# Two feed-forward stages of a one-core kernel: expert and tile numbers are loaded into registers without range checks, and at other places

## The chip, the core and the metric

The kernel runs on one core of a Trainium2 chip. The metric is the device time of one execution in microseconds (us). A core has several engines that run side by side, each with a sequencer that reads its own list of instructions in order: TensorE (PE in the profile; PEld is its loading of weights), VectorE (DVE), ScalarE (ACT), GpSimd (POOL), and SyncE (SP), which only issues transfers. Engines wait for each other by semaphores. A `q` behind an engine's name in the profile (DVEq, PEldq) means its sequencer: what it does by itself, such as arithmetic on registers, and not the engine's data path.

## The reference

Six blocks follow each other on x, an array of 8 x 512 tokens of 128 values: a feed-forward (f), a state-space scan (s), a feed-forward (f), a mixture (m), causal attention (a), and the mixture again (m). The change lies in both feed-forwards, which share weights:

```python
def _L0_ffn_ref(hidden_states, gate_w, w1, b1, w2, b2):
    x = hidden_states.reshape(-1, h)
    gate_probs = jax.nn.softmax(x @ gate_w.T, axis=-1)
    expert_idx = jnp.argmax(gate_probs, axis=-1)
    expert_w = jnp.take_along_axis(gate_probs, expert_idx[:, None], axis=1)[:, 0]
    out = jnp.zeros_like(x)
    for e in range(n_experts):                       # 8
        ye = jax.nn.relu(x @ w1[e] + b1[e]) @ w2[e] + b2[e]
        out = out + jnp.where((expert_idx == e)[:, None], ye * expert_w[:, None], 0.0)
    return out.reshape(b, s, h)
x = x + 0.5 * _L0_ffn_ref(_layernorm(x), ...)
```

Each of the 4096 tokens goes through one of 8 experts, which is known only when the data are there.

## The kernel before

**Sorting.** A feed-forward stage normalises the tokens, writes them to DRAM, computes the gate, and sorts the tokens by expert. The sorted tokens fill 32 tiles of 128. Where a tile holds the tokens of two experts it is worked on twice, so there are 32 + 7 = 39 items, each a pair of an expert and a tile. DVE computes both numbers for all items (`expert_f`, `tile_f`, L646 and L647), writes them as integers to two small rows in SBUF (`expert_of`, `tile_of`) and raises `items_ready` (L649).

**The item loop.** `up(j)` multiplies tile j's tokens by the expert's first weights (four products, L815; each takes two passes, so the profile has eight), `hidden(j)` adds the bias and applies the relu (one quarter on DVE, L671, three on ScalarE, L734), `down(j)` adds the second bias by a product (L823) and multiplies by the second weights (L827), `result(j)` adds the masked product to the sorted results on DVE (L680). DVE also copies each item's first weights to a fixed place, two items ahead (`pick`, L666). `turn_in(t)` transposes a gathered tile (L797), and ScalarE copies it (L724). POOL gathers tiles from DRAM up to eight ahead (`AHEAD`, L853) and scatters finished tiles back by ten items later (L859), one of each in turn, once the loop is under way: gather t waits for the transpose of tile t - 8, and scatter t for the result of item t + 7. When all are scattered, SP reads the rows back and DVE adds them to x (L709).

Each engine has its own order of this, written out by hand: TensorE does `turn_in(j+2)`, `up(j+1)`, `down(j)`; DVE `pick(j+2)`, `hidden(j+1)`, `result(j)`; ScalarE `tokens(j+2)`, `hidden(j+1)`.

**The numbers in registers.** Which weights, bias column and tokens an instruction reads hangs on the item's two numbers, so each engine loads them into registers of its sequencer. `item_values` (L559 to L562) loads four at once, and puts behind the load, for each value, register arithmetic and an assert that it is within 0 and `top`. `choose(j)` calls it when j is a multiple of four, for both numbers on DVE (at the head of `pick`) and on TensorE (at the head of `up`), and for the expert on ScalarE (in `hidden`). With 39 items that is ten times a stage.

The code that the change touches, and what calls it:

Of the kernel before, what the change touches and what calls it, by code (L numbers as in the profile page):

```python
# [17 lines left out]
ALU = mybir.AluOpType  # L18
# [5 lines left out]
T = B * S // P  # L24
# [4 lines left out]
E, F = 8, 512  # L29
FC = F // P  # L30
ITEMS = T + E - 1
# [82 lines left out]
def build(nc, a, consts, rotary, out, xhat_dram, yrow_dram, stages="fsf"):  # L114
    ctx = ExitStack()
    with ctx:
        def sb(name, shape, dt=F32):
            return ctx.enter_context(nc.sbuf_tensor(name, shape, dt))
# [62 lines left out]
        expert_of = sb("expert_of", [1, ITEM_PAD], I32)  # L181
        tile_of = sb("tile_of", [1, ITEM_PAD], I32)
# [232 lines left out]
        def slots_unit_scalar(act):  # L415
            act.wait_ge(mix_set[1], 1)
            nc.scalar.activation(mu_t[:, 1], bank[7][:, 0:SLOTS], ACT.Sqrt).then_inc(mix_set[2], 1)
# [134 lines left out]
        def ffn(n):  # L552

            s, at = ffn_sems, {k: v * stages[:n].count("f") for k, v in FFN_COUNTS.items()}
            stored, gathered, scattered, back = (ffn_rings[k] for k in RING_COUNTS)
            lanes_on_vector = n == 0
            BY_DVE = 1

            def item_values(engine, table, j, top):  # L559

                last = min(j + 4, ITEMS)
                return nc.values_load_multi_w_load_instructions(table[0:1, j:last], engines=[engine.engine], min_val=0, max_val=top)[1]  # L562

            after_finish[n] = lambda dve, g: normalise_vector(dve, n, s, at, g, stored, at["stored"])
            for k, counts in RING_COUNTS.items():
# [16 lines left out]
            def vector(dve):  # L582
                chain = Chain(dve, s["v"], chains["f"])
# [8 lines left out]
                top, esum, prob, first, dest, lane, row, at_token = (r_t[:, k, :] for k in range(8))  # L592
# [42 lines left out]
                expert_f, tile_f, at_row, expert_at = (item_f[:, k, :] for k in range(4))  # L635
# [9 lines left out]
                nc.vector.tensor_scalar(token_of[:], at_token, -1.0, None, ALU.add).then_inc(s["gather_ready"], 1)  # L645
                chain(nc.vector.tensor_reduce(expert_f, item_cmp[:], AX.X, ALU.add))  # L646
                chain(nc.vector.tensor_tensor(tile_f, number, expert_f, ALU.subtract))  # L647
                nc.vector.tensor_copy(expert_of[:, 0:ITEMS], expert_f[0:1, :])
                nc.vector.tensor_copy(tile_of[:, 0:ITEMS], tile_f[0:1, :]).then_inc(s["items_ready"], 1)  # L649

                dve.wait_ge(s["items_ready"], at["items_ready"] + 1)
                picked = {}
                placed = {}

                def choose(j):
                    if j % 4 == 0:
                        for k, e in enumerate(item_values(dve, expert_of, j, E - 1)):
                            picked[j + k] = e
                        for k, t in enumerate(item_values(dve, tile_of, j, T - 1)):
                            placed[j + k] = t  # L660

                def pick(j):
                    choose(j)
                    if j >= 2:
                        dve.wait_ge(s["h_mm"], at["h_mm"] + j - 1)
                    nc.vector.tensor_copy(w1_tile[:, j % 2, :], w1[:, bass.ds(picked[j], 1), :]).then_inc(s["w1_ready"], 1)  # L666
# [6 lines left out]
                    last.then_inc(s["hT_ready"], 1)  # L673

                def result(j):
                    dve.wait_ge(s["y_mm"], at["y_mm"] + j + 1)
                    if j:
                        dve.wait_ge(s["y_ready"], at["y_ready"] + j)
                    rows = y_sorted[:, bass.ds(placed[j] * D, D)]
                    nc.vector.scalar_tensor_tensor(rows, bank[6 + j % 2][:, 0:D], item_mask[:, j:j + 1], rows,  # L680
                                                   ALU.mult, ALU.add).then_inc(s["y_ready"], 1)

                dve.wait_ge(w1_in, 16)
                pick(0)
                pick(1)
                chain(nc.vector.tensor_scalar(at_row, tile_f, float(P), cst[:, C_P1:C_P1 + 1], ALU.mult, ALU.add))
                chain(nc.vector.tensor_tensor(item_cmp[:], over_items(starts), over_breaks(at_row), ALU.is_lt))
# [25 lines left out]
            def scalar(act):  # L713
                normalise_scalar(act, n, s, at, stored, at["stored"])
                act.wait_ge(s["one_ready"], at["one_ready"] + 1)
                nc.scalar.activation(r_log[:], r_exp[:], ACT.Exp).then_inc(s["exp_ready"], 1)
                if n == 0 and "s" in stages:
                    scan_setup_scalar(act)
                if n == early:
                    slots_unit_scalar(act)  # L720

                def tokens(t):
                    act.wait_ge(s["g_turned"], at["g_turned"] + t + 1)
                    nc.scalar.copy(xgT[:, t * P:t * P + P], bank[t % 2][:, 0:P]).then_inc(s["xgT"], 1)  # L724

                picked = {}

                def hidden(j):
                    if j % 4 == 0:
                        for k, e in enumerate(item_values(act, expert_of, j, E - 1)):  # L730
                            picked[j + k] = e
                    act.wait_ge(s["h_mm"], at["h_mm"] + j + 1)
                    for c in range(BY_DVE, FC):
                        last = nc.scalar.activation(hidT[:, j % 2, c, :], bank[4 + j % 2][:, c * P:c * P + P], ACT.Relu,  # L734
                                                    bias=b1T[:, bass.ds(picked[j] * FC + c, 1)])
                    last.then_inc(s["hT_ready_a"], 1)

                if not lanes_on_vector:
                    act.wait_ge(s["row_hot"], at["row_hot"] + 1)
                    nc.scalar.activation(tile_hot[:, 1], tile_hot[:, 2], ACT.Copy, scale=cst[:, C_P1:C_P1 + 1]).then_inc(s["lanes_ready"], 1)  # L740
                act.wait_ge(s["items_ready"], at["items_ready"] + 1)
                tokens(0)
                tokens(1)
                hidden(0)
                for j in range(ITEMS):
                    if j + 2 < T:
                        tokens(j + 2)
                    if j + 1 < ITEMS:
                        hidden(j + 1)

            def tensor(pe):
                if n == stages.index("f"):
                    pe.wait_ge(placed_w, 1)
                for i in range(GROUPS):
# [4 lines left out]
                    for h in range(2):  # L759
                        pe.wait_ge(s["xT_ready"], at["xT_ready"] + 2 * i + h + 1)  # L760
                        for k in range(TB):
                            last = pe.matmul(bank[2][:, (8 * i + 4 * h + k) * E:(8 * i + 4 * h + k + 1) * E], xT[:, h, k * P:k * P + P],  # L762
                                             gateT[:], start=True, stop=True)
# [14 lines left out]
                for t in range(T):  # L778
                    pe.wait_ge(s["hot_ready"], at["hot_ready"] + t + 1)
                    last = pe.matmul(bank[2][:, 0:2 * T], lane_hot[:, t, :], tile_hot[:, 0:2, t, :], start=(t == 0), stop=(t == T - 1))  # L780
# [9 lines left out]
                picked = {}  # L790
                placed = {}
# [4 lines left out]
                        pe.wait_ge(s["xgT"], at["xgT"] + t - 1)  # L796
                    pe.transpose(bank[t % 2][:, 0:P], xg[:, t % AHEAD, :], ident).then_inc(s["g_turned"], 1)  # L797

                def choose(j):
                    if j % 4 == 0:  # L800
                        for k, e in enumerate(item_values(pe, expert_of, j, E - 1)):
                            picked[j + k] = e
                        for k, t in enumerate(item_values(pe, tile_of, j, T - 1)):
                            placed[j + k] = t

                def up(j):
                    choose(j)
                    pe.wait_ge(s["w1_ready"], at["w1_ready"] + j + 1)
                    pe.wait_ge(s["xgT"], at["xgT"] + min(j + 1, T))
                    if j >= 2:  # L810
                        pe.wait_ge(s["hT_ready"], at["hT_ready"] + j - 1)
                        pe.wait_ge(s["hT_ready_a"], at["hT_ready_a"] + j - 1)
                    tokens = xgT[:, bass.ds(placed[j] * P, P)]
                    for c in range(FC):
                        last = pe.matmul(bank[(2 if c < BY_DVE else 4) + j % 2][:, c * P:c * P + P], w1_tile[:, j % 2, c * P:c * P + P], tokens,  # L815
                                         start=True, stop=True)
                    last.then_inc(s["h_mm"], 1)

                def down(j):
                    e = picked[j]  # L820
                    if j >= 2:
                        pe.wait_ge(s["y_ready"], at["y_ready"] + j - 1)
                    pe.matmul(bank[6 + j % 2][:, 0:D], ones3[:], b2rows[:, bass.ds(e * D, D)], start=True, stop=False)  # L823
                    pe.wait_ge(s["hT_ready"], at["hT_ready"] + j + 1)
                    pe.wait_ge(s["hT_ready_a"], at["hT_ready_a"] + j + 1)
                    for c in range(FC):
                        last = pe.matmul(bank[6 + j % 2][:, 0:D], hidT[:, j % 2, c, :], w2[:, bass.ds(e, 1), c, :],  # L827
                                         start=False, stop=(c == FC - 1))
                    last.then_inc(s["y_mm"], 1)
# [11 lines left out]
            def gpsimd(pool):  # L841
# [23 lines left out]
                for j in range(T + LATER):  # L865
                    if j + AHEAD < T:
                        gather(j + AHEAD)
                    if j >= LATER:
                        scatter(j - LATER)

            return dict(sync=sync, vector=vector, scalar=scalar, tensor=tensor, gpsimd=gpsimd)


# [1055 lines left out]
```

## Time and profile before

| | us |
|---|---|
| median of 3 runs | 1026.81 (1023.82 to 1027.28) |
| the profiled execution | 1027.21 |
| its span, of which all shares are | 1025.5 |
| TensorE products busy | 770.5 (75%) |
| DVE busy | 631.1 (62%) |
| ScalarE busy | 523.9 (51%) |
| POOL busy | 419.4 (41%) |
| item loop of the first stage, first up product to last scatter's start | 65.79 to 170.38 |
| item loop of the second stage | 282.93 to 389.32 |

The busy time of an engine counts operations on data only. What a sequencer does by itself shows as idle time of its engine, with "issue" as what ended it where the engine waited for no other, and has rows of its own when one asks for the source line. In brackets behind a row of the timeline stands how long the engine had been idle before it and who ended that. A number such as x8 is how many instructions the row merges.

### The profile page before, as it was taken

How to read it: one execution, taken by the hardware profiler on the slowest of the kernel's cores; microseconds unless marked ns; L12 is line 12 of the kernel's file. 1: busy time of each engine (PE TensorE's matmuls, PEld its weight loads, DVE VectorE, ACT ScalarE, POOL GpSimd, SP SyncE). 2: the span in 40 equal slices, each digit the busy share in tenths (PEclk: the TensorE clock that was granted, in tenths of full speed). 3: DMA queues.
4: the chain of work that ended last, by engine and by line, in shares of the span. 5: the costliest groups of instructions: out<-in, count | busy, mean ns of one | idle time of the engine just before them, and what ended most of it. 6: DMA issues, size and time to landing. Idle time of an engine off the chain costs nothing.

```text
span 1025.5 us, 18801 instructions
## 1 busy us (share of the span) xinstructions
PE 770.5 (75%) x5550; PEld 513.1 (50%) x5550; DVE 631.1 (62%) x2289; ACT 523.9 (51%) x1435; POOL 419.4 (41%) x537
## 2 busy tenths in 40 slices
PE   4768775698378871299784788899899899829977
PEld 3658774457278771177571223333333333317757
DVE  4544333866743346955378677777768787466634
ACT  5324432505134431766611267667667677677660
POOL 2055733301146532411136575675674834251100
PEclk9999998696589996599895579899889999959998
DMA  5731103002011103000003532321422400000002
GB/s 150 233 87 35 53 24 83 21 1 83 10 38 44 41 27 93 1 1 1 2 20 43 63 48 33 48 44 33 54 37 31 64 4 2 3 1 1 1 1 82
DMA packets 52530, 42.03 MB, mean 41 GB/s; under 512 B 9224, under 2 KB 48080, under 8 KB 52432
## 3 DMA queue, kind: packets, MB, share of 16 engines
q1 hardware_dynamic: 46784, 31.74, 15.7%
q0 software_dynamic: 4096, 8.40, 2.8%
q8 instruction: 48, 0.79, 0.3%
q10 hardware_dynamic: 1552, 0.70, 0.3%
q14 instruction: 50, 0.41, 0.1%
HBM read 17.35 MB, written 10.49 MB: 27 GB/s over the span
## 4 chain that ended last, share of the span: by engine, by line
PE 49%; DVE 19%; issue 9%; ACT 8%; POOL 7%; DVEq 4%; DMA 2%; ACTq 1%; SPq 0%; POOLq 0%
PE psum L815 6%; PE psum L827 6%; PE psum L1525 5%; DVEq L562 4%; PE psum L1296 3%; PE psum L1259 3%; PE psum L762 3%; PE psum L1268 3%; DVE half_stats L447 3%; DVE cst L1592 2%; PE psum L1510 2%; DVE x L709 2%; PE psum L1465 2%; PE psum L1359 2%; PE psum L758 2%
## 5 line engine op out<-in xcount | busy, mean ns | idle before, releaser
L1592 DVE CUSTOM_DVE_ANT_0 cst<-psum,rot 128x512 bf16<-128x512 f32 (+3 forms) x512 | 219.0, 487 | 70.5 <-PE psum L1497 61.4
L1654 ACT ACTIVATE arena<-psum 128x512 f32<-128x512 f32 (+1 forms) x384 | 178.3, 530 | 56.2 <-PE psum L1510 50.4
L1497 PE MATMUL psum<-arena 48*128 48x512 bf16 (+3 forms) x512 | 122.2, 330 | 17.0 <-DVE row_max L1592 11.3
L734 ACT ACTIVATE arena<-psum,gate_b1T 128x128 f32<-128x128 f32 x234 | 69.0, 365 | 118.2 <-PE psum L815 118.2
L1510 PE MATMUL psum<-arena 51*128 51x512 bf16 (+3 forms) x512 | 114.8, 315 | 13.7 <-ACT arena L1654 7.1
L815 PE MATMUL psum<-arena 128*128 x624 | 90.2, 291 | 46.4 <-DVE arena L671 33.0
L853 POOL DMA_INDIRECT arena<-xhat_rows,token_of x64 | 62.3, 974 | 121.3 <-DVE token_of L645 81.0
L815 PEld LDWEIGHTS psum<-arena 128*128 128x128 f32 x624 | 81.5, 204 | 51.0 <-issue 51.0
L1525 PE MATMUL psum<-arena 128*32 128x512 f32 (+3 forms) x1024 | 98.7, 484 | 7.6 <-POOL arena L1752 7.6
L1749 POOL TENSOR_SCALAR_AFFINE_SELECT arena<-arena 128x384 f32<-128x384 f32 x128 | 63.6, 521 | 97.5 <-ACT arena L1654 97.5
L827 PE MATMUL psum<-arena 128*128 x624 | 89.0, 287 | 0.5 <-ACT arena L734 0.5
L859 POOL DMA_INDIRECT result_rows<-arena,token_of x64 | 62.9, 983 | 62.6 <-DVE arena L680 50.8
L827 PEld LDWEIGHTS psum<-arena 128*128 128x128 f32 x624 | 78.1, 197 | 2.0 <-issue 0.9
L1510 PEld LDWEIGHTS psum<-arena 51*128 51x128 bf16 x512 | 38.5, 96 | 80.0 <-ACT arena L1654 45.7
L1497 PEld LDWEIGHTS psum<-arena 48*128 48x128 bf16 x512 | 38.9, 98 | 63.1 <-DVE row_max L1592 50.5
L666 DVE COPY arena<-arena 128x512 f32 x78 | 33.1, 426 | 59.1 <-issue 59.1
L469 ACT ACTIVATE st<-st 128x8 f32<-128x8 f32 x24 | 4.9, 208 | 113.2 <-DVE st L461 113.1
L680 DVE SCALAR_TENSOR_TENSOR arena<-psum,item_mask,arena 128x128 f32 x78 | 27.2, 349 | 41.2 <-PE psum L827 41.1
L1252 PE MATMUL psum<-cst,xh 128*128 128x128 f32 x64 | 10.6, 292 | 53.0 <-POOL xh L1136 53.0
L671 DVE TENSOR_SCALAR arena<-psum,gate_b1T 128x128 f32<-128x128 f32 x78 | 27.3, 350 | 36.1 <-PE psum L815 36.0
L1136 POOL TENSOR_TENSOR xh<-arena,st 128x512 f32<-128x512 f32 x16 | 18.9, 1184 | 69.3 <-PE psum L1252 67.5
L447 DVE BATCH_NORM_STATS2 half_stats<-x 128x6 f32<-128x128 f32 x192 | 39.4, 278 | 7.2 <-DMA x<-in_L_attn_x 6.4
(248 smaller groups left out, 1648.3 us busy)
## 6 DMA issues: line engine op xcount, KB each, us to landing
arena<-cut SPq DMA_DIRECT2D x192, 64.0 KB
xhat_rows<-xh SPq DMA_DIRECT2D x16, 256.0 KB, 2.3
arena<-result_rows SPq DMA_DIRECT2D x8, 512.0 KB, 6.0
x<-in_L_attn_x SPq DMA_DIRECT2D x4, 512.0 KB, 7.7
arena<-in_L_ffn_w SPq DMA_DIRECT2D x1, 2048.0 KB, 10.1
out<-x SPq DMA_DIRECT2D x4, 512.0 KB, 3.2
arena<-xhat_rows,token_of POOLq DMA_INDIRECT x64, 2.5
result_rows<-arena,token_of POOLq DMA_INDIRECT x64, 2.3
```

Source lines behind the costliest of these rows:

```text
L447: nc.vector.bn_stats(half_stats[:, t, :], x[:, t, :]).then_inc(stat_sem, 1)
L734: last = nc.scalar.activation(hidT[:, j % 2, c, :], bank[4 + j % 2][:, c * P:c * P + P], ACT.Relu, bias=b1T[:, bass.ds(picked[j] * FC + c, ...
L815: last = pe.matmul(bank[(2 if c < BY_DVE else 4) + j % 2][:, c * P:c * P + P], w1_tile[:, j % 2, c * P:c * P + P], tokens, start=True, sto ...
L827: last = pe.matmul(bank[6 + j % 2][:, 0:D], hidT[:, j % 2, c, :], w2[:, bass.ds(e, 1), c, :], start=False, stop=(c == FC - 1))
L853: pool.indirect_dma_start(xg[:, t % AHEAD, :], None, xhat_dram, bass.IndirectOffsetOnAxis(token_of[:, t:t + 1], 0)).then_inc(gathered[t % ...
L859: pool.indirect_dma_start(yrow_dram, bass.IndirectOffsetOnAxis(token_of[:, t:t + 1], 0), y_sorted[:, t * D:t * D + D], None).then_inc(scat ...
L1497: mm = pe.matmul(to[:, col:col + (k + 1) * P], q_stack[b % STACKS][rows, h, k * P:k * P + P], k_stack[b % STACKS][rows, h, 0:(k + 1) * P], ...
L1510: mm = pe.matmul(bank[MAX_BANKS + number % EXP_BANKS][:, col:col + S - k * P], k_stack[b % STACKS][rows, h, k * P:k * P + P], q_stack[b % ...
L1525: last = pe.matmul(bank[6][32 * j:32 * j + 32, k * P:], v_aug[b % 2][:, k, HALF * a + h, :], prob_e[g % 2][:, j, E_AT[k]:E_AT[k] + S - k * ...
L1592: last = nc.vector.tensor_tensor_reduce(masked_scores[:, number % 2, col:col + n_keys], frm[:, col:col + n_keys], mask[:, S - n_keys:], 1. ...
L1654: nc.scalar.activation(prob_e[g % 2][:, j, first:last], bank[MAX_BANKS + number % EXP_BANKS][:, 0:last - first], ACT.Exp, scale=DH ** -0.5 ...
L1749: pool.affine_select(blocks, blocks, pattern=[[0, 3], [1, P]], compare_op=ALU.is_ge, fill=0.0, base=0, channel_multiplier=-1)
```

## The change

The loads are made with the option that leaves the checks out. For that, tile numbers are clamped to 0 to 31 by one more operation on DVE before they are stored. And the two numbers are loaded at different places: `choose_expert` where j is a multiple of four, `choose_tile` at j = 0 (two values) and then where j mod 4 is 2 (four). On DVE experts are loaded in `pick` as before and tiles in `result`; on TensorE tiles in `up` and experts in `down`; on ScalarE experts in `hidden` as before.

```diff
-            def item_values(engine, table, j, top):
-                last = min(j + 4, ITEMS)
-                return nc.values_load_multi_w_load_instructions(table[0:1, j:last], engines=[engine.engine], min_val=0, max_val=top)[1]
+            def item_values(engine, table, j, last, top):
+                return nc.values_load_multi_w_load_instructions(
+                    table[0:1, j:min(last, ITEMS)], engines=[engine.engine], min_val=0, max_val=top,
+                    skip_runtime_bounds_check_because="an expert is a count of 7 comparisons and a tile is clamped to 0..31 before it is stored")[1]
+            def choose_expert(engine, picked, j):
+                if j % 4 == 0:
+                    for k, e in enumerate(item_values(engine, expert_of, j, j + 4, E - 1)):
+                        picked[j + k] = e
+            def choose_tile(engine, placed, j):
+                if j == 0 or j % 4 == 2:
+                    for k, t in enumerate(item_values(engine, tile_of, j, j + 4 if j else 2, T - 1)):
+                        placed[j + k] = t
...
                 chain(nc.vector.tensor_tensor(tile_f, number, expert_f, ALU.subtract))
+                chain(nc.vector.tensor_scalar(tile_f, tile_f, 0.0, float(T - 1), ALU.max, ALU.min))
...
                 def pick(j):
-                    choose(j)
+                    choose_expert(dve, picked, j)
...
                 def result(j):
+                    choose_tile(dve, placed, j)
                     dve.wait_ge(s["y_mm"], at["y_mm"] + j + 1)
...
                 def up(j):
-                    choose(j)
+                    choose_tile(pe, placed, j)
                     pe.wait_ge(s["w1_ready"], at["w1_ready"] + j + 1)
...
                 def down(j):
+                    choose_expert(pe, picked, j)
                     e = picked[j]
```

The order of instructions shows what stands on the engines. A TENSOR_LOAD is a load of registers, an ISA row register arithmetic or an assert. TensorE before, around up(4): the transpose, both loads with their checks, the up products, the bias product of the item before.

```order
L797 MATMUL psum<-cst,arena 128x128
L562 TENSOR_LOAD expert_of
L562 ISA x8
L562 TENSOR_LOAD tile_of
L562 ISA x8
L815 ISA
L815 MATMUL psum<-arena 128x128 x4
L823 ISA
L823 MATMUL psum<-arena,ones 128x128
```

TensorE in the changed kernel, from up(5) to up(6): experts ahead of the bias product of down(4), tiles ahead of the up products of item 6. Lines of the code are one less for L815 and six more for L797.

```order
L814 ISA
L814 MATMUL psum<-arena 128x128 x4
L561 TENSOR_LOAD expert_of
L823 ISA
L823 MATMUL psum<-arena,ones 128x128
...
L803 MATMUL psum<-cst,arena 128x128
L561 TENSOR_LOAD tile_of
L814 ISA
L814 MATMUL psum<-arena 128x128 x4
```

The 16 ISA rows are gone, and the two loads stand at two places of the loop, two items apart in what they are for. DVE before, around pick(8): both loads, then copy, relu and result.

```order
L562 TENSOR_LOAD expert_of
L562 ISA x8
L562 TENSOR_LOAD tile_of
L562 ISA x8
L666 ISA
L666 COPY arena<-arena 128x512
L671 ISA
L671 TENSOR_SCALAR arena<-psum,gate_b1T 128x128
L680 ISA
L680 SCALAR_TENSOR_TENSOR arena<-psum,item_mask,arena 128x128
```

DVE in the changed kernel at the same place: the copy is L673 here, the relu L678, the result L688.

```order
L561 TENSOR_LOAD expert_of
L673 ISA
L673 COPY arena<-arena 128x512
L678 ISA
L678 TENSOR_SCALAR arena<-psum,gate_b1T 128x128
L561 TENSOR_LOAD tile_of
L688 ISA
L688 SCALAR_TENSOR_TENSOR arena<-psum,item_mask,arena 128x128
```

The experts are still loaded ahead of the copy, and the tiles have moved behind the relu, ahead of the result's wait for the down products.

## Rows read from the trace of the kernel before

**Rows 1.** chain of waits, 44 to 420 us, shares by line

```profile
by line: PE psum L815 17.1%; PE psum L827 15.9%; DVEq L562 10.0%; issue 8.7%; DVE x L709 5.1%; DVE half_stats L447 4.0%; PE psum L762 3.7%; PE psum L939 3.1%; PE psum L758 2.3%; DMA arena<-result_rows 2.2%; DVE arena L680 1.9%; DMA arena<-x
```

**Rows 2.** source line L562: ns min/median/max, first and last start

```profile
L562 DVEq FUSED_REGOPS  x156: 183/183/216, 58.9 to 380.2; - x156
...
L562 DVEq TENSOR_LOAD <-expert_of x20: 339/343/805, 58.3 to 376.8; - x20
```

**Rows 3.** timeline: start us, us, what, [idle before <-releaser]

```profile
93.65 0.35 DVE L680 SCALAR_TENSOR_TENSOR arena<-psum,item_mask,arena 128x128 f32 x1 [0.63 <-PE psum L827]
...
96.79 0.43 DVE L666 COPY arena<-arena 128x512 f32 x1 [2.79 <-issue]
...
97.72 1.15 PE L815 MATMUL psum<-arena 128*128 x8 [2.10 <-DVE arena L671]
...
99.82 1.06 PE L815 MATMUL psum<-arena 128*128 x8
...
100.02 0.35 DVE L680 SCALAR_TENSOR_TENSOR arena<-psum,item_mask,arena 128x128 f32 x1 [0.63 <-PE psum L827]
...
101.83 1.06 PE L815 MATMUL psum<-arena 128*128 x8
```

**Rows 4.** sequencers on L562, L823 and L827, 92.65 to 94.6 us

```profile
L562 DVEq TENSOR_LOAD <-expert_of x1: 343/343/343, 93.7 to 93.7; - x1
...
L562 PEldq TENSOR_LOAD <-expert_of x1: 329/329/329, 94.3 to 94.3; - x1
...
L823 PEldq FUSED_REGOPS  x1: 60/60/60, 92.7 to 92.7; - x1
...
L827 PEldq FUSED_REGOPS  x4: 46/51/60, 93.7 to 94.1; - x4
```

**Rows 5.** first loop's start: timeline, and TensorE's sequencer on L562

```profile
62.31 0.27 ACT L724 COPY arena<-psum 128x128 f32<-128x128 f32 x1 [2.39 <-PE psum L797]
...
L562 PEldq TENSOR_LOAD <-expert_of x1: 529/529/529, 62.3 to 62.3; - x1
...
65.79 2.07 PE L815 MATMUL psum<-arena 128*128 x8 [3.05 <-issue]
...
70.41 1.06 PE L815 MATMUL psum<-arena 128*128 x8
```

**Rows 6.** timeline, end of the first stage's item loop

```profile
162.22 1.15 PE L815 MATMUL psum<-arena 128*128 x8 [2.65 <-DVE arena L666]
...
164.21 1.06 PE L815 MATMUL psum<-arena 128*128 x8
...
166.10 1.06 PE L815 MATMUL psum<-arena 128*128 x8
...
170.38 0.97 POOL L859 DMA_INDIRECT result_rows<-arena,token_of  x1 [0.47 <-DVE arena L680]
```

**Rows 7.** POOL's timeline (gathers 18, 31, scatter 14), and the page's issues

```profile
89.88 0.94 POOL L853 DMA_INDIRECT arena<-xhat_rows,token_of  x1 [3.58 <-PE psum L797]
...
123.67 0.97 POOL L853 DMA_INDIRECT arena<-xhat_rows,token_of  x1 [0.30 <-issue]
...
126.23 0.98 POOL L859 DMA_INDIRECT result_rows<-arena,token_of  x1 [0.30 <-issue]
...
arena<-xhat_rows,token_of POOLq DMA_INDIRECT x64, 2.5
```

**Rows 8.** timeline of TensorE, second stage

```profile
282.93 2.07 PE L815 MATMUL psum<-arena 128*128 x8 [2.83 <-issue]
...
288.18 1.06 PE L815 MATMUL psum<-arena 128*128 x8
...
381.15 1.15 PE L815 MATMUL psum<-arena 128*128 x8 [2.64 <-DVE arena L666]
```

**Rows 9.** busy time by stretch (PE, PEld, DVE, ACT, POOL), granted clock, DMA share

```profile
283.00:300.00 17.00, 14.80 (x98) 14.41 (x99) 7.62 (x18) 6.28 (x23) 9.14 (x10) 0.77 0.14 37
...
320.00:345.00 25.00, 20.75 (x184) 20.17 (x183) 10.53 (x31) 11.66 (x42) 18.45 (x20) 1.00 0.17 51
```

More of the change, by code:

```diff
@@ L653, in vector @@
                 placed = {}
[L655 to L660, printed above, removed]
                 def pick(j):
-                    choose(j)
+                    choose_expert(dve, picked, j)
                     if j >= 2:
@@ L728, in hidden @@
                 def hidden(j):
-                    if j % 4 == 0:
-                        for k, e in enumerate(item_values(act, expert_of, j, E - 1)):
-                            picked[j + k] = e
+                    choose_expert(act, picked, j)
                     act.wait_ge(s["h_mm"], at["h_mm"] + j + 1)
@@ L797, in turn_in @@
                     pe.transpose(bank[t % 2][:, 0:P], xg[:, t % AHEAD, :], ident).then_inc(s["g_turned"], 1)
[L799 to L804, printed above, removed]
                 def up(j):
-                    choose(j)
+                    choose_tile(pe, placed, j)
                     pe.wait_ge(s["w1_ready"], at["w1_ready"] + j + 1)
```

## The prediction, made before the changed kernel ran

> **What bounds the kernel now.** I read the page's chain first, then the chain of waits of the first part of the span (44 to 420 us), which holds both feed-forward stages, then the timeline inside one stage, then the sequencer's rows of the load's line. The chain [rows 1] gives 17.1% to the up products (L815), 15.9% to the down products (L827) and 10.0% to DVE's sequencer on L562, the register load. So TensorE sets the pace, and is stopped by something that is no computation. The timeline [rows 3] shows it: the up products of items start 2.01 us apart (99.82, 101.83), and once in four items there is a hole: DVE idles 2.79 us "issue" before its weight copy at 96.79, TensorE 2.10 us before 97.72.
>
> The load's line says what fills the hole [rows 2]. On DVE one value costs 183 ns of FUSED_REGOPS (plus an assert), and the load itself, of up to four values, costs 343 ns in the median, 805 at most. Eight values and two loads make 8 x 0.18 + 2 x 0.34 = 2.2 us, and small gaps between ten-odd sequencer instructions the rest of the 2.79. TensorE's sequencer goes through the same list at the same time (its load starts at 94.3, one of DVE's at 93.7 [rows 4]), so its 2.10 us of idleness has two causes side by side, and both must go. ScalarE has half of the list (experts alone) and waits for the same up products as DVE; it can only come nearer to being early.
>
> **What the change removes.** Behind the load nothing is left but the load: 8 x 2 instructions less per four items on DVE and TensorE, 8 on ScalarE. DVE loads its experts before the weight copy and its tiles before a result two items later; TensorE its tiles before up(4m+2) and its experts before down(4m). What is left over is one load of some 0.34 us at each of four places, and each needs a cover.
>
> - TensorE, tiles before up(4m+2). The place in the queue is the old one, behind the down products and a transpose; there the sequencer arrived at 94.3 [rows 4], and while the array ran out of work only at 97.72 - 2.10 = 95.6 [rows 3]. The queue is 1.3 us ahead there; I set aside 0.5 for the address and the dispatch, 0.8 are left, and a load of 0.33 fits.
> - TensorE, experts before down(4m). The sequencer had the address of the bias product ready at 92.7 and then stood until 93.7, when the relu values came and L827's addresses follow [rows 4]. One load fits into that 1.0 us.
> - DVE, tiles before result(4m+2). DVE waits 0.63 us for the down products before L680 (at 100.02 [rows 3]), and its sequencer starts a load some 0.05 us after the operation ahead of it has started (93.65 and 93.7 [rows 3, 4]). Covered.
> - DVE, experts before the weight copy. Not covered on DVE itself: the copy starts one load later than in an item without one. From the result's start at 93.65 it would be 0.05 + 0.34 for the load, some 0.15 for the address, and 0.43 for the copy: it ends at 94.6, and TensorE wants it at 95.6. So it costs nothing; the bounds are 0 and 0.34 x 18 = 6 us, and I take 0.
> - The clamp on DVE is one operation of the size of its neighbours, with its chain wait some 0.2 us, ahead of the event that lets the engines load. TensorE has to wait for gather 0 at that time, until its transposes can run, and the first token copy stands at 62.31 [rows 5]. Cost 0, of at most 0.2 in each stage.
>
> The Trainium skill, DMA: Bandwidth & Descriptors, section "Latency and other measured facts", gives a tensor_load a floor of about 600 ns. The trace disagrees here: 343 ns median, though single loads took 805 ns [rows 2]. With 600 ns at each place the covers on TensorE (0.8 and 1.0 us) would still hold and the sum stay, only with less to spare.
>
> **The sum.** Stage 1. At the start TensorE's first load begins at 62.3 and takes 0.53 us [rows 5]; with no checks and one load up(0) starts at about 62.3 + 0.53 + 0.3 = 63.1 instead of 65.79 (0.3 for address and dispatch is an estimate): 2.7 us. Then from up(0) to up(36). Now: 162.22 - 65.79 = 96.4 us [rows 5, 6]. After: up(0) to up(2) as now, 70.41 - 65.79 = 4.6 (the first products run at half speed, 2.07 us for eight against 1.06); 28 items of 2.005 us = 56.1; six without a transpose at 166.10 - 164.21 = 1.89, 11.3. Together 72.0, which is 24.4 less. What follows up(36) stays as it is. 27.1 us for the stage.
>
> Stage 2. 381.15 - 282.93 = 98.2 us [rows 8]; after: 288.18 - 282.93 = 5.25, and the same 56.1 + 11.3: 72.7, 25.5 less. At the start TensorE idled 2.83 us "issue" before up(0), all but 0.1 to 0.2 of it goes: 2.7. 28.2 us.
>
> In these 55 us lie 2 x 9 holes of some 2.4 us (43), the two starts (5.4), and 6.9 from products that run at 1.2 instead of 2.4 GHz after a hole, from the few loads that took 0.8 us, and from longer first products behind a hole (1.15 against 1.06 us [rows 3]): the granted clock is 0.77 in 283:300, where the loop starts and has its first hole [rows 9]. Nothing in the loop lets TensorE idle afterwards, so I count these as gone.
>
> Is something else late next? POOL. It issues one gather and one scatter per item at 2.6 us ((123.67 - 89.88) / 13) [rows 7], slower than TensorE's 2.005, and only the surplus of gathers made before keeps it from being the bound. After the change up(2) is at 67.7 and up(9) at 81.7. Gather 18 waits for the transpose of tile 10, just before up(9), and starts 0.55 us after it: 82.2. Gather 31 starts 13 x 2.6 later, at 116.0, and has landed by about 119.5 (0.97 to issue and 2.5 to land [rows 7]); its transpose stands before up(30), at 67.7 + 56.1 = 123.8. TensorE never waits for it, with 4.3 us to spare. The scatters: number 14 starts 2.56 us after gather 31 (123.67 and 126.23 [rows 7]), 118.6, and 17 more at 1.28 put the last at 140.4 at the earliest. TensorE ends the last up at 67.7 + 56.1 + 8 x 1.89 = 138.9, and the last scatter follows 170.38 - 166.10 = 4.3 later [rows 6], at 143.2. So the results decide, not POOL, by 2.8 us. In stage 2 the distances are alike. Without this bound the gain is complete; with it at its worst it would lose little.
>
> Sum: 27.1 + 28.2 = 55.3 us. The profiled execution took 1027.2 (span 1025.5), 0.4 above the median of 1026.8. 1027 - 55 = **972 us**. Everything behind the stages (reads of the rows, the scan, the mixing, attention) waits for the stage's end and shifts.
>
> **The rivals.**
> - A load is not covered. Then TensorE stands at each: 38 loads inside the loops at 0.4 us give 15 back, 987. For it: single loads take 0.8 us [rows 2]. Against it: sequencer and array run 1 us apart [rows 4]. The skill's floor of 600 ns would bring this case nearer.
> - POOL becomes the bound. If pairs took 2.9 instead of 2.6 us and scatters 1.5, the last scatter would be 3.9 + 3.6 later, less the 2.8 to spare: about 5 us a stage, 982. For it: 2.6 us a pair is little more than the operations themselves, POOL hardly rests between gathers 18 and 31 [rows 7]; against it: the two margins.
> - The slow stretches stay, because the clock falls at other times as well: of the 6.9 us in the sum that are neither holes nor starts, 5 would stay, 977.
> - Slower than before: TensorE runs at half clock for long. An item at 1.2 GHz costs 1.7 us more (eight products 2.07 against 1.06 less overlap, twice an item). Where more than 55 / 1.7 = 32 of the 78 items did so, the gain would be used up; with all of them it is 1027 - 55 + 78 x 1.7 = 1104. For it: the granted clock of 0.77 in one stretch. Against it: in 320:345, with only 2 us holes, it is 1.00 [rows 9]. The Trainium skill, TensorE: Matmul & The Clock Gate, Part 1, says that throttled is the default and that activity releases it; by that a loop without holes is the safer one.
> - The change does not do what it says: the sequencer spends its time on the load although the checks are gone. The order shows the rows gone, and the load has its own row, so this is small: 1025.
>
> **How the numbers follow.** Forecast 0.78 (its own range 968 to 978), an uncovered load 0.07, POOL 0.07, slow stretches 0.05, half clock 0.02, no effect 0.01. The range of 966 to 984 takes in the first, the slow stretches, POOL, and loads of which most are covered; what is left out is about 1 in 10. About 0.3% is what a measurement of this kernel can tell from no change, so faster has 0.97, same 0.01, slower 0.02.
>
> **What would show it.** In the profile after: no FUSED_REGOPS and no assert on the load's line, about 20 fewer microseconds "issue" before the weight copy per stage; up products 2.0 us apart throughout; up(0) at about 63.1; the last scatter of stage 1 at about 143 instead of 170.38, that of stage 2 about 55 us earlier than now; DVE's sequencer gone from the chain; POOL with only its waits for results at the tail. I am wrong if up products wait for gathers, if the granted clock falls in the loop, or if four-item periods stand well above 8.0 us.

## The result, and the profile after

| | before | changed |
|---|---|---|
| median, us | 1027.05 (4 runs) | 977.23 (975.62 to 979.56, 4 runs) |
| ratio | | 0.9514, 95% interval 0.9473 to 0.9555 |
| profiled execution, span | 1025.5 | 975.4 |
| last scatter of stage 1 starts | 170.38 | 147.71 |
| last scatter of stage 2 starts | 389.32 | 342.75 |

The kernel became 50 us faster; forecast were 55, to 972. In the chain that ended last, on the page of the changed kernel, DVE's sequencer has 0%, against 4% before:

```profile
PE 54%; DVE 15%; ACT 9%; POOL 7%; issue 7%; DMA 3%; SPq 2%; ACTq 1%; DVEq 0%; POOLq 0%
```

The timeline of TensorE in the changed kernel, in the middle of the first stage (start, duration, what, idle time before), is to be read against [rows 3]:

```profile
84.89 1.15 PE L814 MATMUL psum<-arena 128*128 x8 [0.15 <-issue]
...
86.99 1.06 PE L814 MATMUL psum<-arena 128*128 x8
...
89.00 1.06 PE L814 MATMUL psum<-arena 128*128 x8
...
91.00 1.06 PE L814 MATMUL psum<-arena 128*128 x8
...
93.41 1.15 PE L814 MATMUL psum<-arena 128*128 x8 [0.24 <-issue]
```

The hole of 2.10 us is gone, but four items take 93.41 - 84.89 = 8.52 us and not the forecast 4 x 2.005 = 8.02. A hole of 0.24 us has stayed, "issue", and the first products behind it take 1.15 us, not 1.06. It stands ahead of the up products of items 4m+2, where the tiles are now loaded. The rows of the load's line say why (duration min/median/max in ns, the first and last start):

```profile
L561 PEldq TENSOR_LOAD <-tile_of x22: 308/1007/1137, 61.8 to 337.7; - x22
...
L561 DVEq TENSOR_LOAD <-tile_of x22: 317/968/1077, 66.9 to 340.7; - x22
...
L561 DVEq TENSOR_LOAD <-expert_of x20: 340/342/754, 58.5 to 332.9; - x20
...
L561 PEldq TENSOR_LOAD <-expert_of x20: 329/332/774, 63.6 to 336.1; - x20
```

Against [rows 2, 4] the loads of experts are what they were. Those of tiles take three times as long, on both engines; before they were as short as those of experts:

```profile
L562 PEldq TENSOR_LOAD <-tile_of x20: 327/333/772, 64.0 to 379.0; - x20
...
L562 DVEq TENSOR_LOAD <-tile_of x20: 340/352/797, 60.1 to 378.8; - x20
```

The load in front of the hole at 93.41 has this row on TensorE's sequencer in the changed kernel:

```profile
L561 PEldq TENSOR_LOAD <-tile_of x1: 1011/1011/1011, 91.9 to 91.9; - x1
```

It began 1.3 us before the array ran out of work, at 93.41 - 0.24 = 93.17, as in [rows 3, 4], and took 1.01 us; the rest is the way from the load's end to the first product, some 0.5 us. The landmarks of the stage, POOL's included:

```profile
62.76 2.07 PE L814 MATMUL psum<-arena 128*128 x8 [0.51 <-ACT arena L732]
...
68.06 1.15 PE L814 MATMUL psum<-arena 128*128 x8 [0.22 <-issue]
...
83.01 0.94 POOL L853 DMA_INDIRECT arena<-xhat_rows,token_of  x1 [1.06 <-PE psum L803]
...
116.62 1.00 POOL L853 DMA_INDIRECT arena<-xhat_rows,token_of  x1 [0.30 <-issue]
...
119.22 1.15 POOL L859 DMA_INDIRECT result_rows<-arena,token_of  x1 [0.30 <-DVE arena L688]
...
147.71 0.97 POOL L859 DMA_INDIRECT result_rows<-arena,token_of  x1 [0.47 <-DVE arena L688]
...
342.75 0.97 POOL L859 DMA_INDIRECT result_rows<-arena,token_of  x1 [0.47 <-DVE arena L688]
```

up(0) started at 62.76 (forecast 63.1). POOL ran as forecast: gather 18 at 83.01 (82.2), gather 31 at 116.62 (116.0), scatter 14 at 119.22 (118.6), and the last scatter waits for DVE's result, not for POOL. The granted clock was 1.00 over the item loop of stage 1, from the first up products on (busy time of PE, PEld, DVE, ACT and POOL, then the clock, as in [rows 9]):

```profile
63.00:148.00 85.00, 81.80 (x693) 78.72 (x693) 40.61 (x115) 43.43 (x148) 58.18 (x60) 1.00 0.17 50
```

### The profile page after: what moved, and what is told of

It reads as the page before. It is cut to its first block, busy times and chain, and to the rows that moved or that the text cites. A ratio compares the mean times of both kernels' runs of the same rounds, so it can differ in the third digit from the quotient of the medians.

```text
span 975.4 us, 18027 instructions
## 1 busy us (share of the span) xinstructions
PE 764.3 (78%) x5550; PEld 507.5 (52%) x5550; DVE 633.9 (65%) x2291; ACT 523.8 (54%) x1435; POOL 419.5 (43%) x537
## 4 chain that ended last, share of the span: by engine, by line
PE 54%; DVE 15%; ACT 9%; POOL 7%; issue 7%; DMA 3%; SPq 2%; ACTq 1%; DVEq 0%; POOLq 0%
PE psum L814 8%; PE psum L827 7%; PE psum L1525 5%; PE psum L1296 3%; PE psum L1259 3%; PE psum L768 3%; PE psum L1268 3%; DVE cst L1592 3%; PE psum L1510 2%; DVE half_stats L447 2%; DVE x L717 2%; PE psum L1359 2%; PE psum L1465 2%; PE psum L1497 2%; ACT arena L1654 2%
## 5 line engine op out<-in xcount | busy, mean ns | idle before, releaser
L1525 PE MATMUL psum<-arena 128*32 128x512 f32 (+3 forms) x1024 | 98.3, 482 | 6.7 <-POOL arena L1752 6.7
L814 PE MATMUL psum<-arena 128*128 x624 | 87.8, 286 | 4.9 <-issue 2.8
L827 PE MATMUL psum<-arena 128*128 x624 | 86.7, 282 | 0.5 <-ACT arena L740 0.5
L814 PEld LDWEIGHTS psum<-arena 128*128 128x128 f32 x624 | 78.9, 199 | 9.8 <-issue 9.6
L827 PEld LDWEIGHTS psum<-arena 128*128 128x128 f32 x624 | 75.8, 192 | 1.8 <-issue 0.9
L688 DVE SCALAR_TENSOR_TENSOR arena<-psum,item_mask,arena 128x128 f32 x78 | 27.3, 351 | 52.8 <-PE psum L827 52.8
L678 DVE TENSOR_SCALAR arena<-psum,gate_b1T 128x128 f32<-128x128 f32 x78 | 27.2, 349 | 28.2 <-PE psum L814 25.9
L1592 DVE DVE_READ_ACCUMULATOR2_ANT row_max<- 128x1 f32 x512 | 42.5, 83 | 0.0
```

The costliest lines, as they stand in the source:

```text
L1525: last = pe.matmul(bank[6][32 * j:32 * j + 32, k * P:], v_aug[b % 2][:, k, HALF * a + h, :], prob_e[g % 2][:, j, E_AT[k]:E_AT[k] + S - k * ...
L1592: last = nc.vector.tensor_tensor_reduce(masked_scores[:, number % 2, col:col + n_keys], frm[:, col:col + n_keys], mask[:, S - n_keys:], 1. ...
```

## The experiments

Four questions: why the tile loads became slow, what each half of the change is worth, whether two engines' checks really hide behind each other, and what a load costs. Medians are of 4 runs each (10 for e7, one run for e8), and the median of before on the same chips was 1026.5 to 1026.6. The up products are L813, L814 or L815, by the kernel. The diffs show the lines that matter, with "..." where others are left out.

**e1: the row of tiles two words later.** Nothing moves in any order; both rows are made four words longer.

```diff
-        expert_of = sb("expert_of", [1, ITEM_PAD], I32)
-        tile_of = sb("tile_of", [1, ITEM_PAD], I32)
+        expert_of = sb("expert_of", [1, ITEM_PAD + 4], I32)
+        tile_of = sb("tile_of", [1, ITEM_PAD + 4], I32)
...
-                nc.vector.tensor_copy(tile_of[:, 0:ITEMS], tile_f[0:1, :]).then_inc(s["items_ready"], 1)
+                nc.vector.tensor_copy(tile_of[:, 2:2 + ITEMS], tile_f[0:1, :]).then_inc(s["items_ready"], 1)
...
-                    table[0:1, j:min(last, ITEMS)], engines=[engine.engine], min_val=0, max_val=top,
+                    table[0:1, j + at_word:min(last, ITEMS) + at_word], engines=[engine.engine], min_val=0, max_val=top,
```

The added argument `at_word` is 2 for tiles and 0 for experts.

> The changed kernel, but the row of tile numbers is stored two words later, so that the loads of four tiles begin at a multiple of four words instead of two words past one. Nothing is moved in any engine's order. Theory (where a load begins): the loads of four tiles cost 0.33 to 0.35 us on TensorE and DVE instead of 1.0, the up products of four items stand 8.0 us apart instead of 8.4 to 8.55, and the time is about 8 us less than the changed kernel's 977, near 969. Rival (the place of the load, beside a busy array and a busy DVE, makes it slow): the loads stay at 1.0 us and the time at 977. A second rival (POOL takes over as soon as the holes go): loads of 0.34, but up products or the last scatter wait for POOL, 972 to 975.

Measured: 967.9 (967.1 to 969.0), ratio to before 0.9428 (0.9386 to 0.9469). The load's line of e1:

```profile
L561 PEldq TENSOR_LOAD <-tile_of x22: 312/330/728, 62.0 to 329.3; - x22
...
L561 DVEq TENSOR_LOAD <-tile_of x22: 337/342/536, 67.2 to 332.6; - x22
```

And its timeline:

```profile
92.01 1.06 PE L814 MATMUL psum<-arena 128*128 x8
...
100.03 1.06 PE L814 MATMUL psum<-arena 128*128 x8
...
143.55 0.97 POOL L859 DMA_INDIRECT result_rows<-arena,token_of  x1 [0.48 <-DVE arena L688]
...
334.61 0.96 POOL L859 DMA_INDIRECT result_rows<-arena,token_of  x1 [0.48 <-DVE arena L688]
```

Loads of 0.33 and 0.34 us, four items in 8.02 us, no hole. So it was not the place of the load in the order that made it slow, but its first word; e2 leaves the rows where e1 has them and moves the experts' first word alone. e1 is the fastest kernel of this study, 9.3 us ahead of the changed one, whose four runs all lie above its four. POOL as the next bound did not appear: the last scatter follows the last result, at 143.55, where the prediction had it (143.2).

**e2: both rows two words later,** so that tiles are loaded from multiples of four and experts are not.

```diff
-                nc.vector.tensor_copy(expert_of[:, 0:ITEMS], expert_f[0:1, :])
+                nc.vector.tensor_copy(expert_of[:, 2:2 + ITEMS], expert_f[0:1, :])
```

> As the one before, but the row of expert numbers is stored two words later as well, so that now its loads of four begin two words past a multiple of four words, and the tiles' do not. Theory (where a load begins): tile loads 0.34 us, expert loads 1.0 us on TensorE, DVE and ScalarE; TensorE's has about 1.0 us of cover and DVE's about 1.0, so the time is 969 to 975. Rival (the place): expert loads stay at 0.33, tile loads at 1.0, 977. If the slow thing is the row of tiles itself, its loads are at 1.0 too.

Measured: 970.9 (970.5 to 971.8). The slowness changed sides with the offset:

```profile
L561 PEldq TENSOR_LOAD <-tile_of x22: 312/336/720, 61.7 to 332.6; - x22
...
L561 DVEq TENSOR_LOAD <-expert_of x20: 794/966/1212, 58.4 to 328.1; - x20
...
L561 PEldq TENSOR_LOAD <-expert_of x20: 765/1003/1131, 63.5 to 330.9; - x20
```

ScalarE's loads of experts went from 0.31 to 0.91 us as well. Nine loads of four became slow in each stage on each of three engines (the tenth is of three values). They cost 3 us here, over e1, and nine slow tile loads on two engines cost 9 us in the changed kernel: at the experts' places there is more cover.

**e3: no checks, both loads together where they stood before.**

```diff
-                if j == 0 or j % 4 == 2:
+                if j % 4 == 0:
...
                 def pick(j):
                     choose_expert(dve, picked, j)
+                    choose_tile(dve, placed, j)
...
                 def up(j):
+                    choose_expert(pe, picked, j)
                     choose_tile(pe, placed, j)
...
```

> No checks and the clamp as in the changed kernel, but both loads stand together where they stood before the change, ahead of the weight copy on DVE and of the up products on TensorE, every fourth item, and begin at multiples of four words. Theory (where a load begins): loads of 0.34 us; two of them are 0.7 us against about 0.8 us of cover on TensorE, so holes of 0 to 0.2 us per four items, 969 to 973: taking the loads apart is worth nothing and costs by its offset. Rival (taking apart is what covers them): holes of 0.4 us or more, 977 or above.

Measured: 974.8 (974.7 to 975.9), ratio 0.9491 (0.9449 to 0.9532). That is between the two expectations (969 to 973, and 977 or above).

```profile
89.13 1.14 PE L815 MATMUL psum<-arena 128*128 x8
...
97.28 1.15 PE L815 MATMUL psum<-arena 128*128 x8
```

Four items take 8.15 us, 0.13 more than in e1, by a start that comes a little late and longer first products; no idle time shows before them. e3 is no slower than the changed kernel: its median is 2.4 us lower, but the runs of the two overlap. Leaving out the checks alone, with the clamp in their place, brings 51.7 us. Taking the loads apart brought nothing as it was done, and 7 us once the tiles begin at a multiple of four (e1).

**e4: checks on, loads taken apart** as in the changed kernel (the option that leaves them out is dropped from the load).

> The changed kernel with the checks behind the loads again; the loads stay taken apart. On TensorE a tile load is then 1.0 + 8 instructions of register work and asserts, about 1.75 us against about 0.8 of cover, an expert load 0.33 + 0.75 against 1.0. Theory (checks and loads cost what their rows show): a hole of 0.9 to 1.3 us per four items, 985 to 995, so of the 50 us gained the move alone would have brought some 35 and the checks the rest. Rival (the checks are all that matters): 1020 or more.

Measured: 1072.9 (1072.0 to 1075.4), ratio 1.0454 (1.0406 to 1.0501): 46 us slower than before. The theory (985 to 995) missed by far. The rival's number, 1020 or more, held, but not its reason: had the checks been all that matters, the time would have come back to that of before, not 46 us over it. The half of the change that brings nothing without checks does harm with them. **e5** is e4 with the offset of e1, to see how much of it is slow loads.

> The kernel of e4 (checks on, loads taken apart) with the row of tiles stored two words later, so that all loads of four cost 0.34 us. e4 took 1072.9, against an expectation of 985 to 995. Theory one (short pieces fit, and only the 1.0 us loads made e4 slow): each piece is 0.34 + 0.75 us on TensorE against 0.8 to 1.0 of cover and 0.34 + 0.85 on DVE, holes of 0.1 to 0.6 us at places, 975 to 1000. Theory two (taken apart, the checks stop DVE, then TensorE, one after the other instead of side by side, and the array falls to its slow clock more often): 1030 to 1060 even with short loads.

Measured: 1040.5 (1038.9 to 1042.9), ratio 1.0146 (1.0119 to 1.0172). Short loads take away 32 of the 46 us, and with them it is still slower than before, within theory two's range. Not all of the 32 is waiting for loads. TensorE's granted clock, which was 1.00 in the changed kernel's loop, fell in both, more in e4. The loop of stage 1 behind its first products, in e5 and then in e4:

```profile
68.00:176.00 108.00, 87.98 (x670) 78.75 (x668) 38.69 (x112) 41.98 (x143) 53.72 (x55) 0.97 0.12 36
...
68.00:193.00 125.00, 96.47 (x675) 86.95 (x673) 37.50 (x113) 42.12 (x144) 54.09 (x55) 0.90 0.11 31
```

Stage 2's loop has the same clock in each: 0.90 in e4 (250 us in both loops together) and 0.97 in e5 (217 us). As an estimate from these, 25 us of full-speed time are missing in e4 and 7 in e5, so up to 18 of the 32 us came by way of the clock. The timeline of DVE and TensorE in e5 around one item 4m+1:

```profile
98.48 0.35 DVE L687 SCALAR_TENSOR_TENSOR arena<-psum,item_mask,arena 128x128 f32 x1 [1.19 <-issue]
...
98.98 0.43 DVE L672 COPY arena<-arena 128x512 f32 x1
...
99.55 1.15 PE L813 MATMUL psum<-arena 128*128 x8
...
101.35 0.23 PE L822 MATMUL psum<-arena,ones 128*128 x1 [0.65 <-issue]
...
104.13 1.15 PE L813 MATMUL psum<-arena 128*128 x8 [1.27 <-DVE arena L672]
```

And two rows of its sequencer on the load's line at that place (count, ns, first and last start):

```profile
L561 PEldq TENSOR_LOAD <-expert_of x1: 329/329/329, 99.7 to 99.7; - x1
...
L561 PEldq TENSOR_LOAD <-tile_of x1: 331/331/331, 102.2 to 102.2; - x1
```

DVE's checks of tiles hold its result back (98.48, 1.19 us "issue") and with it the weight copy at 98.98. It ends at 99.41, and the up products start at 99.55, as soon as it is there: the sequencer has no lead. It then begins the expert load at 99.7 and is through with its checks at 101.2; the array idles 0.65 us before L822. The products of down(4m) follow, and at 102.2 comes the tile load with its checks, 1.5 us more: a hole of 1.27 us. The row names the weight copy, but that had ended at 103.60, 0.53 us before, and the last check only at about 103.65. Before the change both lists ran at one time on both engines, and made one hole of 2.1 us; in this stretch DVE's and TensorE's stand behind each other. How much of the time that is, e9 and e10 are to tell.

**e6 and e7: checks on one engine alone, loads together** (e3 with the option dropped for DVE, or for TensorE).

> Both loads together at the old place, checks off on TensorE and ScalarE, on on DVE alone (e3 with DVE's checks back). Theory (side by side: DVE's 2.8 us and TensorE's list run at the same time, the longer one sets the hole): DVE's list still delays the weight copy and the relu, so a hole of 1.9 to 2.1 us per four items stays, 1012 to 1026. Rival (the two lists add up): about half of e3's gain of 52 us, 1000.

> The mirror of the one before: checks on TensorE alone, off on DVE and ScalarE. Theory (side by side): TensorE's sequencer arrives 1.3 us ahead of the array and needs 2.7 + 0.4 us for its list, so the hole is 1.8 to 2.0 us, 1008 to 1024. Rival (adds up): 1000.

Measured: e6 1018.4 (1017.7 to 1018.8), ratio 0.9924 (0.9900 to 0.9948); e7 1025.2 (1022.9 to 1028.4), 0.9990 (0.9972 to 1.0008). Taking the checks from TensorE is worth 8 us, taking them from DVE nothing that can be told, and both together 52. Side by side is right, though e7 lies 1 us above the theory's 1008 to 1024. Two reservations. ScalarE's checks are off in e6, e7 and e3 alike, and no run has them off alone; in the kernel before, all 118.2 us that ScalarE idled ahead of its relus ended on TensorE's up products, so they were not what it waited for. And the clock takes part: it is 0.97 to 0.98 over the loops behind the first products before, in e6 and in e7, and 1.00 in e3, which by the estimate above is some 5 of the 52 us. In e6 DVE holds the copy back and TensorE waits for it:

```profile
103.06 0.43 DVE L674 COPY arena<-arena 128x512 f32 x1 [2.77 <-issue]
...
103.63 1.15 PE L815 MATMUL psum<-arena 128*128 x8 [1.72 <-DVE arena L674]
```

In e7 the copy is early, and TensorE's own sequencer makes the same hole:

```profile
104.89 0.43 DVE L674 COPY arena<-arena 128x512 f32 x1 [0.54 <-PE psum L815]
...
108.08 1.15 PE L815 MATMUL psum<-arena 128*128 x8 [2.12 <-issue]
```

**e9 and e10: checks on one engine alone, loads apart and at multiples of four** (e1 with the option dropped for one engine).

> The kernel of e1 (unchecked, apart, all loads of four at a multiple of four words, 967.9) with the checks back on DVE alone. e5, with them on all three engines, took 1040.5, 72.6 more. Theory (shared cover: the array lives on the lead of TensorE's sequencer, DVE's pieces of 1.3 us eat some of it, TensorE's pieces the rest, and only both together break it): 970 to 985, and this and the next kernel together have far less than 72 us of excess. Rival (each engine's pieces cost by themselves): about 36 of excess here, 1004.

> The mirror of the one before: checks back on TensorE alone, at its two places, 1.1 us each against covers of 0.8 and 1.0 us. Theory (shared cover): holes of 0.1 to 0.5 us, 970 to 985. Rival (each by itself): 1004.

Measured: e9 990.6 (990.4 to 991.2), ratio 0.9650 (0.9625 to 0.9676), 22.7 over e1; e10 1000.9 (1000.1 to 1002.8), ratio 0.9755 (0.9728 to 0.9783), 33.0 over it. Together 55.7 of the 72.6 of e5. So most of it is each engine by itself: e10 is near the rival's 1004, e9 between the theory and the rival, and my shared cover as the main cause fell. Some 17 us are left for what the lists do together. They have no run of their own, and two more things lie in them: ScalarE's checks, on in e5 alone (3.1 us of ScalarE's idle time there ended on its own sequencer), and the clock, which over the loops is 1.00 in e9 and e10 against 0.97 in e5, about 7 us by the estimate above.

What I had missed is that on TensorE the two places are neighbours: experts ahead of down(4m), then its products, then tiles ahead of up(4m+2). Rows of e10, TensorE and its sequencer:

```profile
L561 PEldq TENSOR_LOAD <-expert_of x1: 330/330/330, 94.4 to 94.4; - x1
...
96.00 0.23 PE L823 MATMUL psum<-arena,ones 128*128 x1 [0.20 <-issue]
...
L561 PEldq TENSOR_LOAD <-tile_of x1: 330/330/330, 96.8 to 96.8; - x1
...
98.78 1.15 PE L814 MATMUL psum<-arena 128*128 x8 [1.26 <-DVE arena L673]
```

The expert list is through at 95.8 and costs a hole of 0.20 us itself. The tile list begins at 96.8, and the array runs out of work at 98.78 - 1.26 = 97.52: a lead of 0.7 us, where it was 1.3 in the changed kernel at the same place. The tile list then takes 1.5 us with its gaps, where I had reckoned 1.1. So part of the second hole, about 0.5 of the 1.26 us, is lead that the first list had used. No run has the checks at one of TensorE's two places alone.

**e8: single loads measured.** 45 loads more on ScalarE behind the first stage's item loop, from the row of experts, with a copy that uses one value of each.

```diff
+                for v in [nc.values_load_multi_w_load_instructions(expert_of[0:1, 8:12], engines=[act.engine], min_val=0, max_val=E - 1, skip_runtime_bounds_check_because='an expert')[1][-1] for _ in range(3 if n == 0 else 0)]:
+                    nc.scalar.copy(probed[:, bass.ds(next(probe_at), 1)], cst[0:1, bass.ds(v, 1)])
...
```

> The kernel of e1 with 45 more register loads on ScalarE after the first stage's item loop, three each of: four values from word 0, 1, 2, 3 and 6 past a multiple of four, one value from word 0 and 1, two from 0, 1, 2 and 3, three from 0, 1, 2 and 3, each followed by a copy of one value, which leaves the kernel's results as they are. Theory (a load that lies within one piece of four words is fast, one that goes over its end is slow): fast (0.3 us) for four from 0, one from 0 or 1, two from 0, 1 or 2, three from 0 or 1; slow (0.9 to 1.0) for four from 1, 2, 3 and 6, two from 3, three from 2 and 3. Rival (any load that doesn't begin at a multiple of four words is slow): also slow one from 1, two from 1 and 2, three from 1. Second rival (a slow load costs by its values: one access of some 0.25 for each): three from 2 costs 0.25 less than four from 2.

Measured: 983.4, one run, 15.5 over e1. The rows shown are, in order: four values from a multiple of four words, four from 1, 2 and 3 words past it, one from 0 and from 1, two from 0, three from 0, three from 3.

```profile
L758 ACTq TENSOR_LOAD <-expert_of x3: 306/307/310, 140.2 to 140.9; - x3
...
L760 ACTq TENSOR_LOAD <-expert_of x3: 909/913/917, 141.5 to 143.4; - x3
...
L762 ACTq TENSOR_LOAD <-expert_of x3: 903/906/953, 144.6 to 146.5; - x3
...
L764 ACTq TENSOR_LOAD <-expert_of x3: 903/911/916, 147.8 to 149.6; - x3
...
L766 ACTq TENSOR_LOAD <-expert_of x3: 286/288/288, 150.8 to 151.5; - x3
...
L768 ACTq TENSOR_LOAD <-expert_of x3: 277/280/280, 152.1 to 152.7; - x3
...
L770 ACTq TENSOR_LOAD <-expert_of x3: 493/493/495, 153.3 to 154.3; - x3
...
L778 ACTq TENSOR_LOAD <-expert_of x3: 701/703/706, 160.8 to 162.3; - x3
...
L784 ACTq TENSOR_LOAD <-expert_of x3: 693/693/696, 168.2 to 169.6; - x3
```

The theory fell, and so did the first rival; the second is right and needs an exception. On ScalarE a load costs by its number of values wherever it begins: 0.28, 0.49, 0.70 and 0.91 us for one to four, 0.21 more for each further one. The one exception is four values from a multiple of four words: they take 0.31, less than two. Two from a multiple of four take 0.49, and two from elsewhere 0.48 to 0.49. This is also what the longest loads of before were [rows 2]: items 36 to 38 are three values, and their loads took 0.70 (ScalarE) to 0.81 us (DVE) before, and 0.70 to 0.89 in the other kernels. The first load of the first stage is longer too, 0.51 to 0.61 us for four values before; why is not tested.

## Why the prediction was right, and where it was 5 us off

- **What stops TensorE.** Right. Without checks, with the clamp and nothing else done, 51.7 us went (e3). That both engines' lists are side by side and both must go is shown by e6 and e7: 8 and 1 us. The prediction also gave the move of the loads a part, as cover for what is left; as made, it brought nothing over e3.
- **The sum.** Stage 1 was to end at 143.2, stage 2 55.3 us earlier. It did so in e1, where the loads have the duration the prediction gave them: 143.55, and 389.32 - 334.61 = 54.7. In the changed kernel it was 147.71, and 46.6 earlier.
- **The step that was off** is the term "one load of some 0.34 us at each of four places". It took the duration of a load of four from the rows of before, where every such load began at a multiple of four words, and put it on tile loads that begin at 2, 6, 10 and so on. They took 1.0 us, three times that, against the 0.8 us of cover that I had left for them on TensorE; the hole of 0.24 us is the difference. The first of the rivals, a load that is not covered, is what happened, at half of the places and for a part of its length; the prediction's price was 15 us for all of them (987), the real one was 9.3 us (977.2 against e1). The change's diff showed the offset; no load of four in the trace of before had one. The rival's argument for itself, single loads of 0.8 us, was a sign of something else, loads of three values (e8).
- **The covers.** Right for loads without checks, as e1 has no hole. Not right as two separate amounts: in e10 the lead at the second place is 0.7 us instead of 1.3, used in part by the list at the first.
- **POOL.** Right to within 0.8 us at three landmarks, and not the bound, in e1 either.
- **The clock.** Right: 1.00 over the loop of stage 1 in the changed kernel, no slow stretch in either loop behind the first products. e4 shows what the half-clock rival would have been about: with holes placed otherwise the mean over its loops is 0.90.
- **The clamp and the start.** Right: up(0) waited for the token copy of ScalarE and started 0.3 us ahead of the forecast. The clamp's own cost wasn't measured apart.
- **Left open.** From the last scatter of stage 2 to the end, with the same code, it takes 636.2 us before, 632.7 changed and 630.8 in e1. This gave 3.5 us back to the forecast, so that it came out nearer (5 us) than its two stages (8.7 us short of 55.3): that is luck. It is also why e1, whose stages went as the sum had them, measured 967.9 and not 972. The start of attention (L1465) comes 137.2 us behind the last scatter before, 137.1 changed and 135.7 in e1; the first products of its L1525 come at 215.2, 213.2 and 211.0. So the changed kernel gains only inside attention, e1 also ahead of it. The cause was not found; these are single executions, and those of the kernel before differ among themselves by up to 8 us (1023.8 to 1031.5), so part of it can be chance.

## What to carry to other kernels

Range checks behind a register load cost more than the load (on TensorE four times 146 + 18 ns before, against 333 ns for a load of four), and as sequencer time they show in no busy column: ask for the sequencer's rows of the line, on every engine that has them, since one engine's list can hide the other's, and taking away one alone brought 8 or 1 us here of 52. Where registers are loaded four at a time, begin at a multiple of four words, and keep it so when loads are moved; take a duration from a profile only for the same number of values and the same first word. Two pieces of sequencer work on one engine that stand within an item draw on one lead: price them together, and test a move of such work by itself: with checks, apart was 14 us slower than together with loads of 0.34 us, and 46 us slower with tile loads of 1.0 us.

## What the runs showed of the hardware that was not expected

- A register load from SBUF takes 0.28 us for one value and 0.21 more for each further one on ScalarE, but 0.31 for four from a multiple of four words (e8). On TensorE and DVE four values took 0.33 and 0.34 from such a word, 1.00 and 0.97 from two words past it (e1, changed).
- The same checks at other places turned a kernel of 1026.6 us into one of 1040.5 with loads of 0.34 us and 1072.9 with tile loads of 1.0 us (e5, e4). The granted clock over the loops behind the first products was 0.97 to 0.98 before, 0.97 in e5 and 0.90 in e4.
